# Softmax sums of 128 columns, a new order of steps at both ends and 47 added products in a gated attention block

## The chip, the cores and the metric

One core of a Trainium2 chip runs the whole kernel. The metric is the device time of one execution in microseconds. Three executions of the kernel before took 727.42, 727.99 and 729.45 us; the median is 727.99.

## What is computed

For 16 sequences of 256 tokens with 512 features, a gated cross-attention with 16 heads of 32 (keys and values from a context of 128 features) and a gated feed-forward net of width 1408, whose inputs and weights are rounded to fp8 values:

```python
scores = jnp.einsum('bhqd,bhkd->bhqk', qh, kh) * inv_sqrt_d
causal = jnp.tril(jnp.ones((sq, sk), dtype=bool))
scores = jnp.where(causal, scores, jnp.finfo(scores.dtype).min)
attn = jax.nn.softmax(scores, axis=-1)
...
x = x + jnp.tanh(g_xattn[0]) * _L0_xattn_ref(_layernorm(x, axis=-1), ctx_512, ...)
x = x + jnp.tanh(g_ffn[0]) * _L0_ffn_ref(_layernorm(x, axis=-1), L0_ffn_w_gate, ...)
...
scale_x = jnp.max(jnp.abs(xr), axis=1, keepdims=True) / FP8_MAX
qx = _fp8(xr / scale_x)
w_scale = jnp.max(jnp.abs(Wr), axis=1, keepdims=True) / FP8_MAX
qw = _fp8(Wr / w_scale)
y = qx * scale_x @ (qw * w_scale).T * scale
```

## The kernel before

The work goes by batches b of 256 tokens, in two halves t of 128. Of each batch, the layer norm of x and the context are split into a high and a low bf16 part and turned by a transposing DMA (`turn_x`). TensorE makes keys, queries and values from them in three bf16 products each. The high and low parts of keys and queries (the low ones made on POOL: `keys_low`, `queries_low`) are stacked by DMAs (`stack_keys(b, i)`, `stack_queries(b, i)`, i = 0 and 1 the high parts, 2 the low part) into K4 and Q4, from which one product gives exact scores.

`scores(b, c)`, for the pair c of heads (8 pairs), makes 768 columns: two heads times three blocks of 128, since of the four blocks of a causal 256 x 256 matrix one is empty. VectorE takes their row maxima (`maxima(b, c)`, L3116) and joins the two blocks of the second half (`second_maxima(b)`, L3121). POOL splits the maxima in three bf16 parts (`max_parts`), TensorE turns them (`turned_maxima`, L1349), ScalarE and a DMA bring them into Q4, and `shifted(b, c)` makes the scores again, transposed and less the maximum. ScalarE takes the exponential into the tile PT (`exps`), POOL clears the upper triangle (`causal_part`, L793), and `weighted(b, g)`, for a group g of four heads, multiplies with the values (L1411) and with `pick` (L1416), whose ones put the sum of the probabilities of head 4g+j into a row of `sum_bank`, a PSUM tile that all four groups add up in. `sums_inverted` (L3125) takes the reciprocal, `inverse_spread` (L3130, L3131) copies the row of each group g to all 32 rows of its block with a stream shuffle, `normalised` (L3136) multiplies, and `projected` makes the output projection. `residual` adds it to x. Then come the second layer norm, the rounding of x, the gate and up products (L1153), silu, the rounding of the product t, the down products, `down_scaled` (L3447), the addition and the store.

The weights of the feed-forward net are made ready ahead of and between the first batches, in 16 units: 0 to 3 are the rows of the down weights (128 x 1408 each), 4 to 15 pairs of 128 rows of gate or up weights. A unit u is loaded (`unit_loaded(u)` on SP's queue, L363 and L365), its row maxima taken on VectorE (`unit_maxima`, L2962), inverted and scaled (`pair_inverse`, `pair_scales`, L2982 and L2989), floored (L2947), lifted (L3056), rounded (L2943 on VectorE, L705 on POOL) and turned by TensorE (`unit_turned`, L1216). The attention weights are split as well (`attention_weights`, low parts on POOL, L779). POOL scatters the turned down rows to DRAM in 11 indirect DMAs (`down_placed`, L673).

The order of all this is written out by hand: for each of the engines and for SP a list of steps, run in order, with a wait on a semaphore in a step where it needs another engine. SP's list starts at L473. Every list has a loop `for k in range(1, 9)` in its middle for the steady batches. A step that waits holds up all behind it in its list. For example, a load of a unit of gate or up weights waits for the VectorE rounding that frees its room:

```python
            unit_loaded(7)
            stack_keys(0, 2)
            stack_queries(0, 0)
```

Here `unit_loaded(7)` waits for the fourth VectorE rounding, and `stack_keys(0, 2)` for the second `keys_low`.

## Time and profile before

| | |
|---|---|
| median of three executions | 727.99 us |
| profiled execution, its own time | 729.19 us |
| its span | 727.4 us |
| mean granted clock of TensorE | 0.978 |
| TensorE busy | 657.9 us (90%), 6091 instructions |
| VectorE busy | 680.1 us (93%), 1127 instructions |
| ScalarE busy | 555.5 us (76%) |
| POOL busy | 538.5 us (74%) |
| chain that ended last | TensorE 47%, VectorE 29%, POOL 11%, DMA 5%, issue 3%, ScalarE 3% |

The span is what the profiler saw from the first to the last instruction; the execution's own time has 1.8 us more around it. Busy shares are means over a beginning in which weights are prepared and batches 0 and 1 run, a steady middle, and an end without new batches. In the rows below PE is TensorE, DVE is VectorE, ACT is ScalarE, and `[2.02 <-DMA Q<-kl]` behind a row says how long the engine had stood idle before it and what released it.

### The profile page before, as it was taken

To read this page: it belongs to the slowest core of one execution; us is meant where nothing else is said; L and a number is where in the kernel's file an instruction comes from. 1 tells how busy PE (TensorE), PEld (TensorE's weight loads), DVE (VectorE), ACT (ScalarE), POOL (GpSimd) and SP (SyncE) were. 2 spreads that over 40 slices of the span, in tenths; PEclk is the share of its full clock that TensorE was granted. 3 is DMA by queue.
4 is the path that set the end of the run, shared out by engine and by line. 5 is a ranking of instruction groups with operands and counts; after the bars stand their busy time and mean duration, and the time that the engine had idled before them with its cause. 6 is when DMAs were issued, how large, how long until landed. Compare 5 with 4: busy or idle time off the path is not lost.

```text
span 727.4 us, 15637 instructions
## 1 busy us (share of the span) xinstructions
PE 657.9 (90%) x6091; PEld 419.9 (58%) x6160; DVE 680.1 (93%) x1127; ACT 555.5 (76%) x995; POOL 538.5 (74%) x601
## 2 busy tenths in 40 slices
PE   1758698999999999999999999999999999998794
PEld 1647476666566666566565657566566556545342
DVE  4999998989899999999999999999999999999997
ACT  6896878987869787878878787979797867555642
POOL 6768889796968778687878686968696677666651
PEclk9888999999999999999999999999999999999997
DMA  8887768385795757585867566675775686512121
GB/s 303 223 153 199 157 147 176 80 176 94 123 158 107 152 105 154 80 181 96 167 108 141 111 144 116 132 144 114 155 123 116 90 150 100 111 22 87 27 70 58
DMA packets 143479, 93.57 MB, mean 129 GB/s; under 512 B 107598, under 2 KB 114126, under 8 KB 143406
## 3 DMA queue, kind: packets, MB, share of 16 engines
q1 hardware_dynamic: 141246, 90.74, 61.6%
q0 software_dynamic: 576, 1.45, 0.8%
q8 instruction: 48, 0.79, 0.5%
q10 hardware_dynamic: 1584, 0.39, 0.3%
q14 instruction: 25, 0.20, 0.1%
HBM read 31.59 MB, written 9.83 MB: 57 GB/s over the span
## 4 chain that ended last, share of the span: by engine, by line
PE 47%; DVE 29%; POOL 11%; DMA 5%; issue 3%; ACT 3%; SPq 0%; ACTq 0%; DVEq 0%
PE pair L1153 26%; DVE mx L3116 5%; POOL PT L793 4%; PE pair L1411 4%; PE pair L1416 3%; DVE room L2943 2%; DVE room L2947 2%; PE pair L1394 2%; DVE room L3260 2%; PE pair L1440 2%; DVE room L3308 2%; PE pair L1436 2%; POOL room L832 2%; DVE tm L3323 2%; DVE wmax L2962 2%
## 5 line engine op out<-in xcount | busy, mean ns | idle before, releaser
L832 POOL TENSOR_TENSOR room<-room,up_scale 128x512 f32<-128x512 f32 (+1 forms) x96 | 125.6, 1312 | 63.1 <-ACT room L2349 62.2
L3116 DVE TENSOR_REDUCE mx<-pair 128x6 f32<-128x768 f32 x128 | 117.6, 947 | 1.7 <-PE pair L1343 1.4
L793 POOL TENSOR_SCALAR_AFFINE_SELECT PT<-PT 128x512 f32<-128x512 f32 x128 | 104.0, 841 | 13.1 <-ACT PT L2274 13.0
L2274 ACT ACTIVATE PT<-pair 128x768 f32<-128x768 f32 x128 | 98.3, 814 | 9.4 <-PE pair L1394 7.8
L1153 PE MATMUL pair<-WgT,room 128*128 128x512 bf16 (+1 forms) x382 | 89.5, 366 | 2.5 <-DVE room L3447 0.8
L1153 PE MATMUL pair<-xT,WqTh 128*128 128x256 bf16 x512 | 86.5, 272 | 1.5 <-ACT WdT L2037 1.3
L1153 PE MATMUL pair<-WuT,room 128*128 128x512 bf16 (+1 forms) x368 | 84.8, 361 | 3.3 <-DVE room L3260 1.4
L2349 ACT ACTIVATE room<-room,sx 128x512 f32<-128x512 f32 (+1 forms) x96 | 65.2, 682 | 24.2 <-DVE room L3260 18.8
L1153 PE MATMUL pair<-WdT,room 128*128 128x512 bf16 x326 | 75.4, 379 | 3.1 <-DMA room<-room 2.9
L2381 ACT ACTIVATE room<-room 128x512 bf16<-128x512 f32 (+1 forms) x96 | 55.8, 586 | 21.2 <-DVE room L3308 21.1
L1153 PE MATMUL pair<-xT,WqTl 128*128 128x256 bf16 x256 | 69.7, 272 | 0.0
L3308 DVE TENSOR_TENSOR room<-pair,room 128x512 f32<-128x512 f32 (+1 forms) x96 | 60.4, 638 | 6.0 <-POOL x L839 2.4
L3260 DVE TENSOR_TENSOR room<-pair,gate_scale 128x512 f32<-128x512 f32 (+1 forms) x96 | 60.3, 637 | 1.9 <-PE pair L1153 1.3
L839 POOL TENSOR_TENSOR x<-room,x 128x512 f32<-128x512 f32 x31 | 44.8, 1445 | 23.3 <-DVE room L3447 23.1
L1153 PEld LDWEIGHTS pair<-WuT,room 128*128 128x128 bf16 x384 | 36.9, 98 | 35.1 <-DVE room L3260 2.0
L1341 PE MATMUL pair<-K,Q 125*128 125x128 bf16 x256 | 51.4, 224 | 6.1 <-DMA Q<-kl 3.6
L1411 PE MATMUL pair<-PT,V 128*32 128x256 f32 (+1 forms) x1024 | 54.3, 329 | 2.4 <-POOL PT L793 2.2
L2943 DVE TENSOR_TENSOR room<-room 128x1408 bf16<-128x1408 f16 (+4 forms) x46 | 55.4, 1205 | 0.2
L1153 PEld LDWEIGHTS pair<-WdT,room 128*128 128x128 bf16 x330 | 31.7, 98 | 40.3 <-issue 2.9
L1153 PEld LDWEIGHTS pair<-WgT,room 128*128 128x128 bf16 x384 | 35.7, 98 | 32.9 <-ACT room L2037 1.8
L1153 PEld LDWEIGHTS pair<-xT,WqTh 128*128 128x128 bf16 x512 | 48.8, 98 | 9.2 <-ACT WdT L2037 1.6
L1416 PE MATMUL pair<-PT,pick 128*32 128x256 f32 (+1 forms) x1024 | 53.5, 326 | 0.0
(151 smaller groups left out, 1863.4 us busy)
## 6 DMA issues: line engine op xcount, KB each, us to landing
xin<-in_x_dram SPq DMA_DIRECT2D x16, 512.0 KB, 4.0
x<-in_x_dram SPq DMA_DIRECT2D x16, 512.0 KB, 4.8
K<-kh SPq DMA_DIRECT2D x32, 256.0 KB, 4.9
Q<-qh SPq DMA_DIRECT2D x32, 256.0 KB, 4.6
out_dram<-x SPq DMA_DIRECT2D x15, 512.0 KB, 3.0
K<-kl SPq DMA_DIRECT2D x16, 256.0 KB, 6.1
Q<-kl SPq DMA_DIRECT2D x16, 256.0 KB, 4.2
room<-in_L_ffn_w_down_dram SPq DMA_DIRECT2D x4, 704.0 KB, 9.0
```

The costliest lines, as they stand in the source:

```text
L793: pool.affine_select(out=view, in_=view, compare_op=ALU.is_ge, fill=0.0, base=0, pattern=[[0, 2], [0, 2], [1, P]], channel_multiplier=-1). ...
L832: pool.tensor_tensor(g, g, up_scale[:, chunk(n)[1]], ALU.mult).then_inc(slw_done, 1)
L1153: last = pe.matmul(out_ap, lhs, rhs, start=(fresh and n == 0), stop=(n == len(terms) - 1), skip_group_check=not fresh)
L1411: pe.matmul(w[HD * j:HD * j + HD, t * P:S], V[:, t, (G * g + j) * HD:(G * g + j + 1) * HD], probabilities(b, 2 * g + j // 2, j % 2, t), st ...
L1416: last = pe.matmul(sum_bank[HD * j:HD * j + HD, t * P:S], pick[:, g, :], probabilities(b, 2 * g + j // 2, j % 2, t), start=(g == 0 and t = ...
L2274: act.activation(head_columns(ring(b, c), 0, 384), head_columns(shifted_pair[c][:, :], 0, 384), ACT.Exp, scale=SCALE).then_inc(exp_done, 1)
L2349: act.activation(g, g, ACT.Silu, scale=sx[:, chunk(n)[0]:chunk(n)[0] + 1]).then_inc(silu_done, 1)
L2381: act.activation(qt[:, t, f], T[:, t, f], ACT.Abs, scale=TOKEN_LIFT).then_inc(abst_done, 1)
L2943: return dve.tensor_tensor(dst, w, high, ALU.subtract)
L3116: dve.tensor_reduce(mx[:, heads, :], head_columns(w, 0, 3 * P).rearrange("p h (r s) -> p h r s", s=P), AX.X, ALU.max).then_inc(max_done, 1)
L3260: dve.tensor_tensor(gs[:, n % 3, 0:width(n)], gate_bank[n][:, 0:width(n)], gate_scale[:, f], ALU.mult).then_inc(gs_done, 1)
L3308: dve.tensor_tensor(T[:, t, f], up_bank[n][:, 0:width(n)], gs[:, n % 3, 0:width(n)], ALU.mult).then_inc(t_done, 1)
```

## The change

1. **The sums.** A group's probabilities are 256 columns for keys of the first half (first and second half of the queries) and 128 columns for keys of the second half. Before, they were summed into a row for 256 queries, by four products of 256 columns and four of 128. Now each of them is summed by products of 128 columns, twelve in a group, into different rows of a `sum_bank` of 128 columns (row 4t + g of a block of 32; `pick` has a matrix for every t and g). The reciprocal works on 128 x 128, and eight stream shuffles of 128 columns spread it.
2. **Products nobody reads.** `kept_busy(b, n)` makes n products of 512 columns into a bank that is overwritten later: 9, 24, 8 and 6 of them, in TensorE's list up to `shifted(0, 0)`. Two explicit waits are ahead of the 24 and the 8.
3. **The order.** Every engine's list and the waits in it are written anew ahead of the loop and behind it. The loops have the same steps in the same order. SP's first loads are x, unit 0, context instead of context, unit 0, x; the residual's x of batch 0 comes much later; `unit_loaded(7)` comes behind `stack_keys(0, 2)`; the stacking of batch 1's low keys comes directly behind its high ones. POOL's `queries_low(1, .)` come ahead of `causal_part(0, 0)`, its scatters later and four in a row ahead of `max_parts(2)`. VectorE's maxima of batch 1 stand together.

The diff, cut to these places (the lists of ScalarE and the parts behind the loops are left out, as are the waits that follow from the order):

```diff
-        pick = sb("pick", [P, KT, HD])
+        pick_flat = sb("pick_flat", [P, TT * KT * (HD + 1)])
...
-        rsum = sb("rsum", [P, S])
+        rsum = sb("rsum", [P, P])
...
+        pick = pick_flat[:, 0:TT * KT * HD].rearrange("p (v c) -> p v c", c=HD)
+        pick_ones = pick_flat[:, :].rearrange("p (v c) -> p v c", c=HD + 1)
...
-            constant(pool.memset(pick[:, :, :], 0.0))
-            for g in range(KT):
-                constant(pool.memset(pick[:, g, :].rearrange("p (a b) -> p a b", b=4)[:, :, g:g + 1], 1.0))
+            constant(pool.memset(pick_flat[:, :], 0.0))
+            for a in range(HD // (TT * KT)):
+                constant(pool.memset(pick_ones[:, :, TT * KT * a:TT * KT * a + 1], 1.0))
...
+            def kept_busy(b, count):
+
+                for _ in range(count):
+                    pe.matmul(bank[b][:, 0:H], identb[:, :], WkvTh[:, 0:H], start=True, stop=True)
+
...
-                for t in range(TT):
-                    for j in range(G):
-                        last = pe.matmul(sum_bank[HD * j:HD * j + HD, t * P:S], pick[:, g, :],
-                                         probabilities(b, 2 * g + j // 2, j % 2, t), start=(g == 0 and t == 0),
-                                         stop=(g == KT - 1 and t == TT - 1), skip_group_check=True)
+                for j in range(G):
+                    pe.matmul(sum_bank[HD * j:HD * j + HD, 0:P], pick[:, g, :], probabilities(b, 2 * g + j // 2, j % 2, 0)[:, 0:P],
+                              start=(g == 0), stop=False, skip_group_check=True)
+                for j in range(G):
+                    pe.matmul(sum_bank[HD * j:HD * j + HD, 0:P], pick[:, KT + g, :], probabilities(b, 2 * g + j // 2, j % 2, 0)[:, P:S],
+                              start=False, stop=False, skip_group_check=True)
+                for j in range(G):
+                    last = pe.matmul(sum_bank[HD * j:HD * j + HD, 0:P], pick[:, KT + g, :], probabilities(b, 2 * g + j // 2, j % 2, 1),
+                                     start=False, stop=(g == KT - 1), skip_group_check=True)
...
-                dve.reciprocal(rsum[:, :], sum_bank[:, 0:S]).then_inc(rsum_done, 1)
+                dve.reciprocal(rsum[:, :], sum_bank[:, 0:P]).then_inc(rsum_done, 1)
 
             def inverse_spread(b, h):
                 if h == 0:
                     dve.wait_ge(rsum_done, b + 1)
-                dve.stream_shuffle(out=R[:, 2 * h, :], in_=rsum[:, :], mask=[2 * h] * HD)
-                dve.stream_shuffle(out=R[:, 2 * h + 1, :], in_=rsum[:, :], mask=[2 * h + 1] * HD).then_inc(r_spread, 1)
+                for g in range(2 * h, 2 * h + 2):
+                    for t in range(TT):
+                        last = dve.stream_shuffle(out=R[:, g, tok(t)], in_=rsum[:, :], mask=[KT * t + g] * HD)
+                last.then_inc(r_spread, 1)
...
             load_w_kv()
+            load_x(0)
+            unit_loaded(0)
             load_c(0)
-            unit_loaded(0)
-            load_x(0)
             unit_loaded(1)
             unit_loaded(2)
             unit_loaded(3)
             load_w_q()
-            load_x1(0)
-            load_c(1)
             turn_x(0, 0)
             load_x(1)
             turn_x(0, 1)
+            load_c(1)
             load_w_out()
             unit_loaded(5)
+            stack_keys(0, 0)
+            stack_keys(0, 1)
+            unit_loaded(4)
             unit_loaded(6)
-            stack_keys(0, 0)
-            unit_loaded(4)
-            stack_keys(0, 1)
+            stack_keys(0, 2)
             unit_loaded(7)
-            stack_keys(0, 2)
             stack_queries(0, 0)
-            load_c(2)
-            turn_x(1, 0)
             stack_queries(0, 1)
             stack_queries(0, 2)
+            turn_x(1, 0)
+            load_c(2)
             turn_x(1, 1)
-            unit_loaded(8)
             load_x(2)
             unit_loaded(9)
+            unit_loaded(8)
             unit_loaded(10)
             stack_keys(1, 0)
             unit_loaded(11)
             stack_keys(1, 1)
+            stack_keys(1, 2)
             stack_queries(1, 0)
+            stack_queries(1, 1)
             load_c(3)
-            stack_keys(1, 2)
+            load_x1(0)
+            unit_loaded(14)
+            no_maxima(2)
+            stack_queries(1, 2)
...
             attention_weights_low(1)
-            x_low(0, 1)
+            attention_weights_low(5)
+            attention_weights_low(3)
             attention_weights_low(4)
-            attention_weights_low(5)
             attention_weights_low(2)
-            attention_weights_low(3)
+            keys_low(0, 0)
             scales1(1)
-            keys_low(0, 0)
             keys_low(0, 1)
             c_low(1)
             x_low(1, 0)
             queries_low(0, 0)
+            queries_low(0, 1)
             x_low(1, 1)
-            queries_low(0, 1)
+            attention_weights_low(7)
             unit_rounded(5)
+            unit_rounded(7)
             keys_low(1, 0)
-            unit_rounded(7)
-            down_placed(2)
-            attention_weights_low(8)
+            keys_low(1, 1)
             c_low(2)
-            down_placed(0)
-            keys_low(1, 1)
             max_parts(0)
             scales1(2)
             unit_rounded(9)
+            x_low(2, 0)
+            queries_low(1, 0)
+            queries_low(1, 1)
...
             keys(0, 0)
+            keys(0, 1)
+            kept_busy(2, 9)
+            unit_turned(1)
+            values(0, 0)
             unit_turned(2)
-            keys(0, 1)
-            unit_turned(1)
             attention_weights(9)
-            values(0, 0)
+            queries(0, 0)
             unit_turned(0)
-            queries(0, 0)
             queries(0, 1)
+            attention_weights(7)
             queries(0, 2)
             queries(0, 3)
+            attention_weights(8)
             unit_turned(3)
+            spread(1)
             values(0, 1)
-            attention_weights(8)
             attention_weights(6)
-            spread(1)
-            attention_weights(7)
-            spread(2)
-            unit_turned(4)
+            pe.wait_ge(v_done, 2)
+            kept_busy(2, 24)
             scores(0, 0)
             scores(0, 1)
-            unit_turned(6)
+            scores(0, 2)
+            spread(2)
+            scores(0, 3)
+            unit_turned(4)
             keys(1, 0)
-            scores(0, 2)
-            scores(0, 3)
             keys(1, 1)
             scores(0, 4)
             scores(0, 5)
             unit_turned(5)
+            pe.wait_ge(w_taken, 5)
+            kept_busy(1, 8)
...
             queries(1, 3)
+            kept_busy(5, 6)
             shifted(0, 0)
...
             unit_maxima(4)
+            put_keys(0)
             pair_inverse(2)
-            put_queries(1)
+            unit_maxima(6)
             pair_scales(2)
-            unit_maxima(6)
-            unit_floored(4)
-            unit_lifted(4)
             unit_maxima(7)
-            unit_rounded(4)
             pair_inverse(3)
             pair_scales(3)
...
             unit_floored(11)
             unit_lifted(11)
+            unit_maxima(14)
             sums_inverted(0)
             inverse_spread(0, 0)
             inverse_spread(0, 1)
...
             maxima(1, 1)
             maxima(1, 2)
             maxima(1, 3)
-            unit_maxima(14)
             maxima(1, 4)
             maxima(1, 5)
-            unit_maxima(12)
-            pair_inverse(6)
             unit_maxima(15)
             maxima(1, 6)
+            pair_inverse(7)
             maxima(1, 7)
+            pair_scales(7)
+            second_maxima(1)
```

How the steps stand in the engines' queues, at three places. First SP's queue from the output projection's weights on; `room<-in_L_ffn_w_gate_dram` and `..._up_dram` are the loads of units 5 (gate), 6 (up), 4 (gate) and 7 (up). Before:

```order
L365 DMA room<-in_L_ffn_w_gate_dram 128x2x512 [waits w_round_dve]
L365 DMA room<-in_L_ffn_w_up_dram 128x2x512 [waits w_round_dve]
L428 DMA K_0<-kh 32x4x1024 [waits kh_done]
L365 DMA room<-in_L_ffn_w_gate_dram 128x2x512 [waits w_round_dve]
L428 DMA K_0<-kh 32x4x1024
L365 DMA room<-in_L_ffn_w_up_dram 128x2x512 [waits w_round_dve]
L428 DMA K_0<-kl 32x4x1024 [waits kl_done]
L437 DMA Q_0<-qh 32x4x1024 [waits qh_done]
```

Now:

```order
L363 DMA room<-in_L_ffn_w_gate_dram 128x2x512 [waits w_round_dve]
L420 DMA K_0<-kh 32x4x1024 [waits kh_done]
L420 DMA K_0<-kh 32x4x1024
L363 DMA room<-in_L_ffn_w_gate_dram 128x2x512 [waits w_round_dve]
L363 DMA room<-in_L_ffn_w_up_dram 128x2x512
L420 DMA K_0<-kl 32x4x1024 [waits kl_done]
L363 DMA room<-in_L_ffn_w_up_dram 128x2x512 [waits w_round_dve]
L433 DMA Q_0<-qh 32x4x1024 [waits qh_done]
```

The last of these loads, unit 7, stood ahead of `K_0<-kl` with its wait for kl_done and stands behind it now.

Second, VectorE from the normalisation of batch 0 to the second maxima of batch 1 (`mx<-mx`); `wmax<-room` are the maxima of units, `mx<-pair` those of scores. Before:

```order
L3136 TENSOR_TENSOR R<-pair,R 128x512 [waits r_spread] x2
L3116 TENSOR_REDUCE mx<-pair 128x2x3 [waits s_made] x4
L2962 TENSOR_REDUCE wmax<-room 128x2 [waits unit_in14]
L3116 TENSOR_REDUCE mx<-pair 128x2x3 [waits s_made] x2
L2962 TENSOR_REDUCE wmax<-room 128x2 [waits unit_in12]
L2982 RECIPROCAL winv<-wmax 128x3 [waits w_maxima]
L2962 TENSOR_REDUCE wmax<-room 128x1 [waits unit_in15]
L3116 TENSOR_REDUCE mx<-pair 128x2x3 [waits s_made] x2
L2989 TENSOR_SCALAR wmult<-winv 128x1 [waits w_inverse]
L2989 TENSOR_SCALAR wmult<-winv 128x1 x2
L3121 TENSOR_TENSOR mx<-mx 128x16 [waits max_done]
```

Now:

```order
L3276 TENSOR_TENSOR R<-pair,R 128x512 [waits r_spread] x2
L3254 TENSOR_REDUCE mx<-pair 128x2x3 [waits s_made] x6
L3091 TENSOR_REDUCE wmax<-room 128x1 [waits unit_in15]
L3254 TENSOR_REDUCE mx<-pair 128x2x3 [waits s_made]
L3113 RECIPROCAL winv<-wmax 128x3 [waits w_maxima]
L3254 TENSOR_REDUCE mx<-pair 128x2x3 [waits s_made]
L3133 TENSOR_SCALAR wmult<-winv 128x1 [waits w_inverse]
L3133 TENSOR_SCALAR wmult<-winv 128x1 x2
L3259 TENSOR_TENSOR mx<-mx 128x16 [waits max_done]
```

Two maxima of units (14 and 12) and one set of scales moved out from between the maxima of scores.

Third, TensorE in the first `weighted(0, 0)`, products with values and with `pick`. Before:

```order
L1411 MATMUL pair<-PT,V 32x256 [waits exp_done,cut_done]
L1411 MATMUL pair<-PT,V 32x256 x3
L1411 MATMUL pair<-PT,V 32x128 x4
L1416 MATMUL pair<-PT,pick 32x256 x4
L1416 MATMUL pair<-PT,pick 32x128 x4
```

Now:

```order
L1455 MATMUL pair<-PT,V 32x256 [waits cut_done,exp_done]
L1455 MATMUL pair<-PT,V 32x256 x3
L1455 MATMUL pair<-PT,V 32x128 x4
L1459 MATMUL pair<-PT,pick_flat 32x128 x4
L1462 MATMUL pair<-PT,pick_flat 32x128 x4
L1465 MATMUL pair<-PT,pick_flat 32x128 x4
```

The four sum products of 256 columns became eight of 128; the value products stay.

## Rows read from the trace of the kernel before

**Rows 1.** The windows by stage: stretch, its length, then busy us (instructions) by engine, clock, DMA

```profile
13.47:69.56 56.09, 36.69 (x289) 30.73 (x292) 55.18 (x75) 47.57 (x77) 42.16 (x34) 0.85 0.85 218
69.56:178.61 109.05, 97.88 (x1037) 66.71 (x1050) 102.16 (x171) 88.64 (x157) 91.56 (x99) 0.98 0.68 138
178.61:489.38 310.77, 305.74 (x2921) 196.28 (x2952) 294.02 (x497) 253.25 (x463) 242.59 (x273) 1.00 0.69 130
...
628.75:727.40 98.65, 79.16 (x514) 38.69 (x521) 92.11 (x169) 47.91 (x87) 50.00 (x48) 0.94 0.23 62
...
50.24:60.48 10.24, 7.83 (x57) 6.68 (x57) 10.21 (x16) 5.95 (x9) 4.50 (x3) 0.50 0.80 197
```

**Rows 2.** The chain that ended last, in order of time: start us, us, what

```profile
226.33 2.38 PE pair L1153 x11
...
264.80 2.38 PE pair L1153 x11
```

**Rows 3.** The timeline of TensorE: start us, us, what, [idle before <-releaser]

```profile
49.99 1.82 PE L1235 MATMUL pair<-ident,wmax 128*128 128x128 f32 x8 [2.79 <-ACT WoTh L2037]
...
54.69 0.29 PE L1341 MATMUL pair<-K,Q 125*128 125x128 bf16 x1 [2.02 <-DMA Q<-kl]
```

**Rows 4.** Windows of the sums' products (L1416) alone, in batch 6

```profile
314.87:315.30 0.43, 0.42 (x8) 0.27 (x12) 1.00 0.38 76
315.30:315.52 0.22, 0.22 (x12) 0.13 (x4) 1.00 1.02 208
```

**Rows 5.** VectorE groups by form: count | busy us, mean ns | idle before

```profile
L3125 DVE RECIPROCAL rsum<-pair 128x256 f32<-128x256 f32 x16 | 28.1, 1755 | 11.4 <-PE pair L1416 11.4
...
L2982 DVE RECIPROCAL winv<-wmax 128x4 f32<-128x4 f32 x4 | 0.7, 172 | 0.1
```

**Rows 6.** The timeline of VectorE: two shuffles of batch 6

```profile
319.22 0.45 DVE L3131 STREAM_SHUFFLE R<-rsum 128x256 f32<-128x256 f32 x1
...
319.57 0.45 DVE L3130 STREAM_SHUFFLE R<-rsum 128x256 f32<-128x256 f32 x1
```

**Rows 7.** The timeline of VectorE: maxima of batch 1

```profile
90.97 0.96 DVE L3116 TENSOR_REDUCE mx<-pair 128x6 f32<-128x768 f32 x1
93.06 2.90 DVE L3116 TENSOR_REDUCE mx<-pair 128x6 f32<-128x768 f32 x3 [1.14 <-PE pair L1343]
95.87 1.21 DVE L2962 TENSOR_REDUCE wmax<-room 128x2 f32<-128x1024 f32 x1
...
100.06 0.66 DVE L2962 TENSOR_REDUCE wmax<-room 128x1 f32<-128x512 f32 x1
...
102.36 0.27 DVE L2989 TENSOR_SCALAR wmult<-winv 128x1 f32<-128x1 f32 x3
102.55 0.17 DVE L3121 TENSOR_TENSOR mx<-mx 128x16 f32<-128x16 f32 x1
```

**Rows 8.** The timeline of TensorE: the end

```profile
706.63 2.54 PE L1153 MATMUL pair<-WuT,room 128*128 128x512 bf16 x12
713.77 0.61 PE L1538 MATMUL pair<-identb,room 128*128 128x128 bf16 x4 [4.59 <-DVE room L2943]
```

**Rows 9.** The timeline of VectorE: the start

```profile
11.08 1.22 DVE L2952 COPY Q<-rows_q 29x4096 bf16<-29x4096 bf16 x1 [1.09 <-POOL rows_k L866]
```

**Rows 10.** Line L365 (loads of gate and up units) from 30 to 50 us

```profile
DMA to landing us min/median/max: 4.6/4.7/4.7
```

**Rows 11.** The timeline of SP

```profile
42.00 0.56 SPq L428 DMA_DIRECT2D K<-kl  x1
```

**Rows 12.** The timeline of POOL

```profile
24.87 9.64 POOL L779 TENSOR_TENSOR WqTl<-x,WqTh 128x512 bf16<-128x512 f32 x4 [4.47 <-ACT WqTh L2037]
```

**Rows 13.** The timeline of VectorE: the preparation of units 4 to 7

```profile
42.36 1.56 DVE L2947 TENSOR_SCALAR room<-room,wmult 128x512 bf16<-128x512 bf16 x2
...
45.28 1.21 DVE L2962 TENSOR_REDUCE wmax<-room 128x2 f32<-128x1024 f32 x1
```

**Rows 14.** Line L673 (scatters of the down rows)

```profile
L673 POOL DMA_INDIRECT placed_down<-WdT,index x11: 963/1005/1124, 62.9 to 143.4; - x11
```

More of the change, by code:

```diff
@@ L834, in added @@
             def added(b, t):
+                if t == 0 and b == 0:
+                    pool.wait_ge(y_done, 1)
+                if t == 0 and b == 9:
+                    pool.wait_ge(y_done, 19)
                 if t == 0 and b >= 12:
@@ L944, in _ @@
             normalised_low(1, 1)
+            keys_low(3, 0)
             c_low(4)
-            keys_low(3, 0)
-            down_placed(9)
+            keys_low(3, 1)
+            down_placed(1)
+            down_placed(10)
+            down_placed(2)
+            down_placed(3)
+            max_parts(2)
             up_scaled(0, 0)
-            max_parts(2)
             up_scaled(0, 1)
+            scales1(4)
             up_scaled(0, 2)
-            keys_low(3, 1)
-            down_placed(10)
-            scales1(4)
+            queries_low(3, 0)
             up_scaled(0, 3)
+            up_scaled(0, 4)
             causal_part(2, 0)
@@ L975, in _ @@
             up_scaled(1, 0)
+            keys_low(4, 1)
             up_scaled(1, 1)
@@ L978, in _ @@
             up_scaled(1, 2)
+            scales1(5)
             up_scaled(1, 3)
-            keys_low(4, 1)
+            queries_low(4, 0)
+            queries_low(4, 1)
             up_scaled(1, 4)
-            scales1(5)
-            up_scaled(1, 5)
             causal_part(3, 0)
@@ L3860, in _ @@
             rounded_x(13, 1)
+            maxima(15, 0)
             sums_inverted(14)
```

2143 lines of the change are left out of this document (1125 added, 1018 removed).

## The prediction, made before the changed kernel ran

> **What bounds the kernel now.** The page's shares have TensorE and VectorE both busy for nine tenths of the span or more, which does not say which of them ends a wait. So I read the windows by stage, then the chain of waits, then single stretches. The windows tell the stages apart [rows 1]. From 13.47 to 69.56 VectorE works 55.18 of 56.09 us and TensorE 36.69: the preparation of weights on VectorE sets the pace. From 69.56 to 178.61 both have gaps, 11.17 us on TensorE and 6.89 on VectorE. From 178.61 to 489.38, batches 3 to 10, TensorE works 305.74 of 310.77 and VectorE has 16.75 us to spare: TensorE sets the pace, and the chain there is one row of products per turn, 38.47 us apart (226.33 to 264.80) [rows 2]. After 628.75, in the last batches, both have gaps again. The granted clock is 1.00 in the middle, 0.85 in the preparation and 0.50 from 50.24 to 60.48 [rows 1]; 0.50 is the level of 1.2 GHz, which followed two waits of TensorE, the later of them for the stacked queries [rows 3].
>
> The profiled execution took 729.19 us (span 727.4 and 1.8 around it), 1.2 above the median of three, 727.99. The sum is made against 729.19, and the result then taken from the median. A difference of 0.3%, 2.2 us, is about what a measurement of this kernel can tell from none.
>
> **1. Softmax sums of 128 columns.** Per group of four heads TensorE now issues 24 records in place of 16 (each product here leaves two). In columns nothing changes: before, two wide and two narrow rounds of four products side by side, 2 x 256 + 2 x 128 = 768 columns; now 6 x 128 = 768. Rows bear out that a record's time goes by columns: eight wide records fill 0.43 us, and 0.22 us hold the eight narrow ones (the row counts 12, since four before them reach in) [rows 4]. So the 0.43 + 0.22 = 0.65 us per group stays, cost 0. If a record cost the same whatever its width, 0.65 / 16 = 0.041 us, 24 would take 0.98, and 64 groups would cost +20.8 us: the upper bound, kept as a rival.
>
> VectorE gains. The reciprocal of 128x256 takes 1.755 us, that of 128x4 0.172 [rows 5]: 0.0063 us a column, so 128x128 takes 0.96, and 0.80 is saved in each of 16 batches. The four shuffles start about 0.345 us apart (319.22, 319.57), 1.38 for all [rows 6]. No row shows one of 128 columns. Bounds: purely by columns eight cost the same, purely by instruction +1.38. Small instructions follow each other every 0.09 us (three in 0.27 [rows 7]); with 0.09 of each 0.345 fixed, eight take 8 x (0.09 + 0.128) = 1.74, +0.36. Net per batch -0.44, between -0.80 and +0.58; I take -0.44, nearest to the column side, since 0.345 for 256 columns is itself far above 0.09. The Trainium skill (Perfetto Trace Analysis, Optimizing Scalar/DVE Operations) speaks against splitting: about 60 ns of overhead per VectorE instruction on SBUF; by that figure four more cost 0.24, and the net would be an estimated -0.56. No row here shows the overhead by itself.
>
> What is it worth? In batches 3 to 10 VectorE already has 16.75 us to spare [rows 1]: 0, hidden behind TensorE; that cover would have to go first. In the last four batches the reciprocal stands between the last sums and the projection, with both engines short of work: 4 x 0.44 = 1.8 us. The epilogue's other swaps change who waits by fractions in 19.5 us of TensorE gaps after 628.75 [rows 1], of which one wait alone, for VectorE's rounding, is 4.59 [rows 8]; nothing shortens that rounding. I give them -0.7; bounds 0 (they only permute) and -2.5. **Epilogue: -2.5.**
>
> **2. Products nobody reads.** 47 of 512 columns. Twelve products of 512 columns take 2.54 us at full clock [rows 8], 0.212 each, so 10.0 us in all. All stand in waits: the nine behind keys(0, 1) and the 24 ahead of scores(0, 0), where TensorE waited 2.79 and 2.02 us [rows 3]; the rest ahead of a wait too. They run in order, so 24 x 0.212 = 5.1 us are free only if their release (v_done) comes 5 us before the stacked queries. What they could give is the clock: 50.24 to 60.48 at 0.50, where TensorE works 7.83 us and VectorE 10.21 of 10.24 [rows 1]. VectorE is the bound there, so a faster TensorE gives nearly nothing in that stretch: 0. Bounds: -1.0, and +5.1 if the 24 delay the scores entirely.
>
> **3. First down unit earlier.** On SP's queue it now stands behind x0 (512 KB) where it stood behind c0 (128 KB), so it is not fetched earlier at all: the change does not do what its name says here. Behind its maximum VectorE stood 1.09 us, until 11.08, for a constant of POOL [rows 9]. There is room for a landing 1.09 us later, and I cannot tell from a row how much later it will be. 0; bounds 0 and +1.
>
> **4. Unit 7 behind a wait.** Before, SP issued unit 7 and then waited for kl_done with K_0<-kl; such a load lands 4.6 to 4.7 us after its issue [rows 10]. Now K_0<-kl stands ahead, and unit 7 queues behind its wait on POOL's keys_low(0, 1). The wait ended and the issue began at 42.00, and took 0.56 [rows 11]. The first of POOL's two key steps now stands ahead of the layer norm's scale steps, so I put kl_done at 40 to 42. Plus 0.6 for the issue and 4.7 for the landing: 45.3 to 47.3. VectorE, whose floor and lift of unit 4 moved behind this maximum (2.97 us, 42.36 to 45.28), asks at 42.3 for what came up at 45.28 before [rows 13]. Idle 3 to 5 us, of which the moved 2.97 are the earlier asking; the net delay is 0 to 2.0 and I take **+1.0**.
>
> **5. From the sums of batch 0 to the second maxima of batch 1.** Before, VectorE took 11.58 us from 90.97 to 102.55, with a wait of 1.14, three unit maxima (1.21, 1.21, 0.66) and small scale steps between the eight maxima of 0.865 [rows 7]. In the new order one unit (0.66) is left between, the others stand ahead or behind: 8 x 0.865 + 0.66 + 0.45 = 8.0 us, **-3.6**, if TensorE and the stacked queries keep up. They are meant to: K_1<-kl is issued right behind the high keys, where it stood behind a wait for the queries and a load of context, and POOL's queries_low(1, .) come ahead of the first causal parts instead of behind the sixth and eighth. This is a move, not a saving: units 12 and 13 are paid later, in the 6.89 us of VectorE gaps of the stage [rows 1]. Bounds: 0 if the whole is paid back, -6.9 if every gap of the stage closes as well. Four of the scatters of down rows now stand in a row ahead of max_parts(2): POOL spends 1.0 us on each [rows 14], and it had 17.5 us of gaps in the 109.05 [rows 1]: 0, bound +2, half of the four.
>
> **Sum:** epilogue -2.5, products 0, unit 7 +1.0, batch 1 -3.6, steady turns 0: -5.1. 729.19 - 5.1 = 724.1 for the profiled execution, and from the median 727.99 - 5.1 = **722.9**.
>
> **Rivals.**
> - *Unit 7 makes it slower.* If kl_done comes later than I think, VectorE stands still with nothing behind it on its queue that could go ahead. The sum crosses zero when unit 7 lands 5.1 us beyond the 46.3 assumed, at 51.4; that is kl_done at 46.1. With kl_done at 48.6, 2.5 us beyond, the time is 730.5. For it: four low parts of the query weights at 2.41 us stand ahead on POOL, and their waits on ScalarE moved. Against: POOL had 4.47 us idle before them [rows 12], and kl_done came at 42.00. Chance 0.09.
> - *No change.* The batch 1 gain is paid back by units 12 and 13 and by scatters on POOL, since from 178.61 on TensorE sets the pace and only its own products count; the epilogue keeps the reciprocals, -1.8, of which half is hidden, -0.9: 727.1. For it: TensorE lacked only 11.17 us in the stage, with the steady pace directly behind. Chance 0.18.
> - *More than forecast.* The clock stays up from 50 to 60 us, so scores(0, .) come sooner, and all of VectorE's 6.89 us of gaps in the stage close: -6.9, with the reciprocals of batches 0 and 1 -0.9, the epilogue -2.5, unit 7 +1.0, in all -9.3: 718.7. Against: VectorE lacked only 0.91 us in the preparation [rows 1], so a sooner TensorE finds it busy. Chance 0.20.
> - *Records cost by number.* +20.8 on the sum: 743.7. Against it is the narrow half of [rows 4]. Chance 0.01. The Trainium skill (TensorE: Matmul & The Clock Gate, "Wait — 56ns, not 53.3ns?") has two floors for small products: about 25 ns from start to start, and about 62 ns each when the sequencer's microcode decodes them. By the second, 24 x 0.062 = 1.49 us per group, an estimated +54 us; the rows, 16 in 0.65 us, are already faster than it allows. By the first, 0.60 us, below the 0.65 kept here.
>
> **Numbers.** The forecast has 0.52. Its own range is -8 to -2.5: 720.0 to 725.5. With the larger gain and the no-change case, each with a spread of 1.3 to 1.5, the range becomes 717.5 to 728.5; outside it are the slower cases (0.10) and tails of the others. Faster by over 2.2 us: 0.52 + 0.20 = 0.72; same 0.18; slower 0.10.
>
> **What would show it.** Right: reciprocals of 128 columns near 0.96 us and shuffles near 0.22 apart; sums of a group still 0.65 us; 38.5 us from turn to turn; second maxima of batch 1 near 99 us instead of 102.55; a landing of unit 7 at 45 to 47. Wrong: VectorE idle over 5 us before unit 7's maximum; turns longer than 38.47, then the sums cost TensorE; the distance to the first steady turn unchanged, then the start was only permuted; products nobody reads ending after the data they wait for.

## The result and the profile after

The changed kernel is slower: 732.11 us (median of 7) against 728.02 us (median of 7 of before, on the same chip), a ratio of 1.0051 with the interval 1.0038 to 1.0065. The forecast was 722.9, and its range ended at 728.5. The profiled execution took 732.13 us with a span of 730.4, 3.0 us above the span before.

I compare by the starts of `turned_maxima(b)` on TensorE, "mark b" below, in us from the span's start. Mark 3 is where the steady turns begin, mark 11 where they end.

| profiled kernel | mark 0 | mark 1 | mark 2 | mark 3 | mark 11 | mark 11 to the end |
|---|---|---|---|---|---|---|
| before | 69.6 | 104.0 | 139.7 | 178.6 | 489.4 | 238.0 |
| changed | 69.1 | 103.5 | 142.5 | 181.5 | 489.6 | 240.8 |

Up to mark 1 the change gains half a microsecond, and then loses 3.3 to mark 2. The steady part hides this in this pair: its turns are 38.49 (38.47 before), but the profiled execution of before had two longer turns (40.1 and 39.9) that the changed one did not have. The end, from mark 11 on, costs 2.8.

The windows by stage, of the changed kernel, in the order of [rows 1] (cut at its own marks; columns as there). The last row is a stretch in the new end:

```profile
13.47:69.06 55.59, 41.79 (x332) 30.86 (x333) 51.97 (x74) 47.55 (x79) 38.08 (x31) 0.97 0.85 202
69.06:181.50 112.44, 101.77 (x1151) 69.24 (x1152) 103.06 (x197) 88.22 (x157) 92.02 (x102) 0.97 0.75 145
181.50:489.60 308.10, 308.09 (x3209) 202.02 (x3208) 291.51 (x561) 253.16 (x463) 241.50 (x272) 1.00 0.68 130
...
631.50:730.40 98.90, 78.61 (x549) 38.91 (x547) 90.30 (x186) 47.43 (x86) 49.53 (x46) 0.94 0.24 55
50.24:60.48 10.24, 8.50 (x87) 6.40 (x86) 10.24 (x17) 6.39 (x11) 4.25 (x2) 1.00 0.98 176
637.33:640.74 3.41, 3.41 (x13) 1.63 (x14) 3.36 (x4) 0.26 (x2) 2.03 (x2) 0.50 0.00 0
```

The preparation runs at a granted clock of 0.97 instead of 0.85, and 50.24 to 60.48 at 1.00 instead of 0.50: the products nobody reads hold the clock here (`no_fill` below has the stretch back without them). In other profiles of the same order one stretch of 3.4 us at 1.2 GHz is left, 47.9 to 51.3 in `after_c5`. The steady part is pure TensorE, 308.09 of 308.10 us. From 69 to 181 VectorE has 9.38 us of gaps where it had 6.89 [rows 1]. From 637.33 to 640.74 TensorE works without a gap at 1.2 GHz; before ran at full clock there, but had such a stretch from 691.9 to 695.4 that the changed kernel did not have.

VectorE's groups by form, against [rows 5] (the line of the reciprocal is L3263 now, of the shuffles L3270), and two of the shuffles in the timeline, against [rows 6]:

```profile
L3263 DVE RECIPROCAL rsum<-pair 128x128 f32<-128x128 f32 x16 | 15.3, 956 | 10.8 <-PE pair L1465 10.7
```

```profile
89.55 0.29 DVE L3270 STREAM_SHUFFLE R<-rsum 128x128 f32<-128x128 f32 x1
...
89.76 0.30 DVE L3270 STREAM_SHUFFLE R<-rsum 128x128 f32<-128x128 f32 x1
```

The chain in the steady part has the sums of a group as three rows of 0.22 us:

```profile
195.29 0.22 PE pair L1459 x8
195.51 0.22 PE pair L1462 x8
195.73 0.22 PE pair L1465 x8
```

Here the forecast held: 0.956 us, shuffles 0.21 apart, 0.65 us per group. So did the landing of unit 7: VectorE waits for it until 46.92 (forecast 45.3 to 47.3).

The loss between marks 1 and 2 begins in the next rows. First VectorE in the changed kernel at 108 us (L3049 is the floor, L3283 the residual), and what TensorE waits for (L1428 is `shifted(1, 4)`, whose bank is that of the output projection):

```profile
107.97 5.78 DVE L3049 TENSOR_SCALAR room<-room,wmult 128x512 bf16<-128x512 bf16 x2
113.67 0.74 DVE L3283 SCALAR_TENSOR_TENSOR x<-pair,tanh_g,x 128x512 f32<-128x512 f32 x1
```

```profile
114.48 0.23 PE L1428 MATMUL pair<-Q,K 99*128 99x128 bf16 x1 [3.86 <-DVE x L3283]
```

The two floors take 5.78 us; the first takes 0.34 (107.97 to 108.31), the second 5.52. Behind TensorE's wait of 3.86 us its clock falls beside full work. That stretch of the changed kernel, and the whole way from mark 1 to mark 2 in the changed kernel and in before:

```profile
115.10:118.50 3.40, 3.40 (x27) 1.88 (x29) 3.11 (x5) 2.76 (x5) 1.42 (x2) 0.50 0.05 5
103.50:142.50 39.00, 33.63 (x379) 22.71 (x379) 33.87 (x64) 29.66 (x56) 29.88 (x36) 0.96 0.62 111
104.00:139.70 35.70, 32.54 (x352) 22.12 (x356) 33.07 (x54) 29.73 (x55) 30.24 (x33) 1.00 0.68 138
```

So TensorE is idle for 5.37 us between the marks where it was idle for 3.16, and busy for 33.63 where it was busy for 32.54: together the 3.3 us. The 3.40 us at 1.2 GHz alone cost about 1.7 us, an estimate from half the clock. POOL in the same stretch:

```profile
107.65 1.25 POOL L673 DMA_INDIRECT placed_down<-WdT,index  x1 [0.17 <-ACT qh L2108]
108.94 2.27 POOL L774 TENSOR_TENSOR kl<-exact,qh 128x512 bf16<-128x512 f32 x2
111.17 0.66 POOL L723 TENSOR_TENSOR xcat<-cin,xcat 128x256 bf16<-128x256 f32 x1
111.79 2.45 POOL L819 TENSOR_SCALAR_AFFINE_SELECT PT<-PT 128x512 f32<-128x512 f32 x4
```

POOL ran seven tensor steps without a gap, from 108.94 to 114.24, the causal parts at 0.61 us each, and VectorE's second floor ended only at 113.75, after six of them. In the kernel before, POOL's row at this place was as dense, but the two took turns: five causal parts in 5.87 us, 1.17 each, and no VectorE step beside the row above 2.2 (POOL first, then VectorE):

```profile
114.13 5.87 POOL L793 TENSOR_SCALAR_AFFINE_SELECT PT<-PT 128x512 f32<-128x512 f32 x5
```

```profile
111.84 1.31 DVE L2947 TENSOR_SCALAR room<-room,wmult 128x512 bf16<-128x512 bf16 x2
113.08 2.17 DVE L2943 TENSOR_TENSOR room<-room 128x1024 bf16<-128x1024 f32 x1
115.17 1.12 DVE L3056 SCALAR_TENSOR_TENSOR room<-room,wmult 128x512 f32<-128x512 f32 x1
```

### The profile page after: what moved, and what is told of

It is laid out like the page before. It is cut to its first block, busy times and chain, and to the rows that moved or that the text cites. A ratio compares the mean times of both kernels' runs of the same rounds, so it can differ in the third digit from the quotient of the medians.

```text
span 730.4 us, 16944 instructions
## 1 busy us (share of the span) xinstructions
PE 671.0 (92%) x6719; PEld 432.1 (59%) x6719; DVE 675.2 (92%) x1255; ACT 553.9 (76%) x995; POOL 540.2 (74%) x601
## 4 chain that ended last, share of the span: by engine, by line
PE 59%; DVE 18%; POOL 11%; ACT 6%; DMA 3%; issue 2%; SPq 1%; ACTq 0%; DVEq 0%
PE pair L1183 32%; PE pair L1455 5%; PE pair L1492 3%; PE pair L1493 3%; PE pair L1488 2%; PE pair L1429 2%; DVE room L3049 2%; POOL PT L819 2%; DVE room L3455 2%; DVE mx L3254 2%; PE pair L1376 2%; PE pair L1378 2%; PE pair L1377 2%; DVE room L3508 2%; PE pair L1428 1%
## 5 line engine op out<-in xcount | busy, mean ns | idle before, releaser
L858 POOL TENSOR_TENSOR room<-room,up_scale 128x512 f32<-128x512 f32 (+1 forms) x96 | 127.2, 1331 | 62.8 <-ACT room L2439 62.5
L2366 ACT ACTIVATE PT<-pair 128x768 f32<-128x768 f32 x128 | 98.4, 815 | 13.7 <-PE pair L1429 8.7
L1183 PE MATMUL pair<-WuT,room 128*128 128x512 bf16 (+1 forms) x384 | 88.3, 361 | 0.7 <-DVE rsum L3263 0.5
L828 POOL TENSOR_TENSOR ol<-R,oh 128x512 bf16<-128x512 f32 x32 | 36.6, 1157 | 26.5 <-ACT oh L2108 26.5
L1428 PE MATMUL pair<-Q,K 99*128 99x128 bf16 x256 | 48.7, 223 | 7.3 <-DVE x L3283 3.9
L1376 PE MATMUL pair<-K,Q 125*128 125x128 bf16 x256 | 49.9, 220 | 5.7 <-DVE R L3276 4.2
L1183 PEld LDWEIGHTS pair<-WdT,room 128*128 128x128 bf16 x330 | 31.9, 98 | 39.2 <-DMA room<-room 2.8
L869 POOL TENSOR_TENSOR x<-room,x 128x512 f32<-128x512 f32 x31 | 42.4, 1369 | 16.1 <-DVE room L3584 16.1
```

Of the source, the lines that this page charges most:

```text
L858: pool.tensor_tensor(g, g, up_scale[:, chunk(n)[1]], ALU.mult).then_inc(slw_done, 1)
L1183: last = pe.matmul(out_ap, lhs, rhs, start=(fresh and n == 0), stop=(n == len(terms) - 1), skip_group_check=not fresh)
L1376: pe.matmul(w[:, tok(4 * h)], q[0:MASK_END, head, 0:P], k[0:MASK_END, head, 0:P], start=True, stop=True)
L1428: pe.matmul(w[:, tok(4 * h)], K4[b % 2][0:99, head, P:S], Q4[b % 2][0:99, head, P:S], start=True, stop=True)
L2366: act.activation(head_columns(ring(b, c), 0, 384), head_columns(shifted_pair[c][:, :], 0, 384), ACT.Exp, scale=SCALE).then_inc(exp_done, 1)
```

## Experiments

My theory: the sums gain a little; the new order ahead of the loop loses about 3 us through the held floor; the new order behind it loses as much again. The rivals: the sums' extra instructions cost it, or one of the two ends alone, or the way the moved loads meet the transposing DMAs.

**The reference.** All kernels of this section have the 92 transposing DMAs replaced by plain ones of the same bytes. The tiles are then not turned, so these kernels compute something else in the same steps:

```diff
-                sp.dma_start_transpose(xT[:, :, tok(t)], xcat[:, t, :]).then_inc(xT_in, 16)
+                sp.dma_start(xT[:, :, tok(t)], xcat[:, t, :].rearrange("p (k s) -> p k s", s=P)).then_inc(xT_in, 16)
```

> The kernel before with each of its 92 transposing DMAs replaced by a plain DMA of the same tile and the same bytes (pieces of 256 bytes), so the operands of the products are not turned; all else is the same. It is the reference for the runs that follow, which have the same replacement. Turns of 38.5 us in the middle as before, the whole within 5 us of 728.0, since TensorE and VectorE set the pace and a copy should land about as fast as a transposition (3.4 to 3.8 us in the trace).

Measured: 727.87 us (10 runs) against 727.58 of the kernel before, ratio 1.000 (0.9987 to 1.0013); turns of 38.47. The replacement is neutral for before, and what follows can be read against before itself.

**The change taken apart.** `after_c5` is the changed kernel. `sums_c5` is before with the sums alone. `begin_c5` has the sums, the changed lists ahead of the loop (with the waits that belong to them) and before's lists behind it; `end_c5` the reverse. The loops are the same in both kernels. The cut in each engine's list:

```diff
 # begin_c5, every engine
+            <list of the changed kernel>
             for k in range(1, 9):
                 ...
-            <list of the changed kernel>
+            <list of the kernel before>
```

> The changed kernel with the same replacement (each of the 92 transposing DMAs a plain copy of the same bytes). The kernel before with it took 727.9 us, as without it (727.6). Theory 1 (the new orders cost the time through TensorE's wait for VectorE at 114 us and through the end, not through the transpositions): 3 to 5 us above that, 731 to 733, again with one VectorE floor of several us beside a row of POOL steps near 108 us. Rival (the loss lies in how the transpositions meet the moved loads and stacking DMAs): within 1 us of 727.9.

> With the same replacement: sums of 128 columns, the changed order ahead of the loop (with its 47 products nobody reads), the order of before behind the loop. Theory 1 (the first part loses near 3 us where one VectorE floor stood 5.5 us beside POOL and TensorE waited 3.9 us for it; the end loses about as much again): 729 to 731, the floor long again. Rival 1 (the whole loss is in the end): 726.4 to 727.9. Rival 2 (the sums cost it all): as after_c5.

> With the same replacement: sums of 128 columns, the order of before ahead of the loop, the changed order behind it. Theory 1: the end alone costs, 729 to 730.5. Rival 1 (the end costs all): as after_c5. Rival 2 (the end costs nothing, the beginning all): 726.4 to 727.9.

> With the same replacement: the sums of 128 columns alone (products, reciprocal, eight shuffles), every order as before. Theory 1 (the two new orders cost the time, the sums gain a little in the last batches): 726 to 727.5. Rival (the eight more products of a group and the four more shuffles cost more than the shorter reciprocal gives): 730 to 732.

| kernel | median us (runs) | ratio to before (interval) | mark 1 | mark 2 | mark 11 to the end |
|---|---|---|---|---|---|
| before_c5 | 727.9 (10) | 1.0000 (0.9987 to 1.0013) | 104.6 | 140.3 | 239.2 |
| after_c5 | 732.1 (8) | 1.0056 (1.0042 to 1.0071) | 104.2 | 143.4 | 241.0 |
| begin_c5 | 733.7 (4) | 1.0079 (1.0059 to 1.0098) | 104.3 | 144.3 | 238.6 |
| end_c5 | 730.8 (9) | 1.0023 (1.0006 to 1.0039) | 107.4 | 143.4 | 240.1 |
| sums_c5 | 725.7 (10) | 0.9974 (0.9953 to 0.9996) | 104.1 | 143.3 | 237.6 |

The changed kernel is as slow with plain copies, so the rival of the transposing DMAs falls. The sums alone are a gain, so the first rival falls too. Added to the sums alone, each new order costs: with the new beginning it is 733.7 (729 to 731 was expected), with the new end 730.8, against 725.7. The two do not add up (8.0 and 5.0 against the 6.4 of both), and behind the new beginning the new end shows no cost in the times: after_c5 is 1.6 below begin_c5, with intervals that overlap.

Executions of one kernel differ by 6 to 7 us here (sums_c5: 723.7 to 729.8), and the profiled ones of sums_c5 and end_c5 took 729.4 and 735.0, which shows in their marks 1 and 2; so a mark of one profile counts only where it repeats. In sums_c5 TensorE waited 1.73 and 2.04 us near 121 and 125, then worked at 1.2 GHz from 126.7 to 130.1, and the distance from mark 1 to mark 2 is 39.2 without a held step; in the same kernel once more (`sums_again` below) it is 35.3. What repeats: the held floor, 5.52 us in the changed kernel, after_c5 and begin_c5 and in no kernel with the old beginning; and, less clearly, the end, 240.1 and 241.0 us with the new lists, 238.6 and 237.6 with the old.

**The held floor.** `residual_first` moves the residual ahead of it; `scatter_between` leaves VectorE alone and moves one of POOL's scatters (`down_placed(0)`, 1.25 us) between the two `queries_low(2, .)`. Both are read against `after_again`, the changed kernel with the plain copies once more.

```diff
 # residual_first, VectorE
+            residual(0, 1)
             unit_floored(12)
-            residual(0, 1)
 # scatter_between, POOL
-            down_placed(0)
             queries_low(2, 0)
+            down_placed(0)
             queries_low(2, 1)
```

> The changed kernel with the plain copies once more, as the reference of this call: 731 to 733 us, with the VectorE floor of 5.52 us and TensorE's wait of 3.9 to 4.0 us behind it, as in three profiles so far.

> after_again with one VectorE step moved: residual(0, 1) ahead of the floors of unit 12. Theory 1 (a VectorE floor that meets a row of POOL steps without a gap is held until the row has a gap, and TensorE waits since the residual stands behind it): the second product of the projection is ready near 109.5 us, the residual ends near 110.3, TensorE's wait of 3.9 us goes, the floors behind it are held again but end at the same time as before (near 114), about 3.5 us long; total 3 to 4 us less, 728 to 729.5. Rival (the wait is only passed on, since TensorE meets the next wait for POOL or VectorE): within 1 us of after_again.

> [...] Theory 1 (the floor is held as long as POOL's row of tensor steps has no gap): the floor gets in during the scatter and takes 0.5 to 2 us instead of 5.52, TensorE's wait of 3.9 shrinks below 1, total 2.5 to 4 less. Rival 1 (the floor is slow for a reason of its own, such as a late input): still 5.5 long, total unchanged. Rival 2 (a POOL scatter holds VectorE just as tensor steps do): still over 4 long.

Measured: after_again 732.7 (6 runs, 732.0 to 737.3; floor 5.52, wait 4.01), residual_first 732.5 (6 runs), scatter_between 733.5 (4 runs). Neither gained, where I had expected 2.5 to 4 us. What failed is the expected total, not the place. In residual_first TensorE's wait of 3.9 is gone, the floor is held 4.61 us and ends at 116.1, and TensorE waits later, for VectorE's maxima(2, 0), again with 3.4 us at 1.2 GHz behind it (126.5 to 129.9):

```profile
111.47 5.25 DVE L3049 TENSOR_SCALAR room<-room,wmult 128x512 bf16<-128x512 bf16 x2
```

```profile
125.91 1.18 PE L1270 MATMUL pair<-ident,wmax 128*128 128x128 f32 x6 [4.37 <-DVE mx L3254]
```

In scatter_between both floors are through by 110.01, the second in 0.34 us beside the scatter, but the lift behind the residual is held in its place (5.33 of the 6.95 us of the two):

```profile
108.50 1.50 DVE L3049 TENSOR_SCALAR room<-room,wmult 128x512 bf16<-128x512 bf16 x2
...
110.85 6.95 DVE L3198 SCALAR_TENSOR_TENSOR room<-room,wmult 128x512 f32<-128x512 f32 x2
```

```profile
109.76 1.11 POOL L673 DMA_INDIRECT placed_down<-WdT,index  x1 [0.16 <-issue]
110.89 1.17 POOL L774 TENSOR_TENSOR kl<-exact,qh 128x512 bf16<-128x512 f32 x1
112.01 0.68 POOL L723 TENSOR_TENSOR xcat<-cin,xcat 128x256 bf16<-128x256 f32 x1
112.63 4.62 POOL L819 TENSOR_SCALAR_AFFINE_SELECT PT<-PT 128x512 f32<-128x512 f32 x7
```

So a floor is not slow by itself: in these three orders whichever of these VectorE steps came up beside POOL's row was held, through six or seven of POOL's steps. It was not held to the end of the row: in the changed kernel the floor ended at 113.75 and the row at 114.24, in residual_first at 116.08 and 116.57. Nor does a scatter let every step through: in the changed kernel the second floor came up at 108.23, with 0.68 us of a scatter still to run, and was held all the same. What ends the holding is open. The Trainium skill (SBUF — State Buffer, "SBUF: two separate sides") says that VectorE and GpSimd share a port pair as an exclusive lock, that the loser is fully blocked for the whole instruction, and that a VectorE operation takes part in it when it is in a two-port mode, or has two SBUF inputs while the GpSimd step reads SBUF. The trace agrees with the blocking and shows more: here VectorE was blocked for six GpSimd steps in a row, 4.7 us, where before it got in after one.

`gaps` puts scatters into the row, on top of residual_first:

```diff
-            down_placed(5)
             x_low(3, 0)
-            down_placed(0)
             queries_low(2, 0)
+            down_placed(5)
             queries_low(2, 1)
+            down_placed(0)
             c_low(3)
             causal_part(1, 0)
             causal_part(1, 1)
+            down_placed(9)
             causal_part(1, 2)
...
             unit_rounded(13)
-            down_placed(9)
```

> residual_first with three of POOL's scatters put between its tensor steps: x_low(3, 0), queries_low(2, 0), scatter, queries_low(2, 1), scatter, c_low(3), two causal parts, scatter. Theory (VectorE steps get in where POOL's row has a scatter): no VectorE step above 2.7 us between 100 and 125, the time from turned_maxima(1) to turned_maxima(2) falls from 39.2 to 39.6 us to 37 to 38.5, total 1 to 2 below the 732.1 to 732.7 of after. Rival (the time lies in VectorE's deferred unit maxima and their floors, not in the held step): 39 or more, total as before.

Measured: 729.9 (10 runs), ratio 1.0022 (1.0003 to 1.0041), where after_c5 has 1.0056 (1.0042 to 1.0071) and residual_first 1.0063 (1.0037 to 1.0088). From mark 1 to mark 2 it takes 37.8 us instead of 39.2 to 39.6, and the longest VectorE step there is 2.60. The expectation came true, the total by a little more. So 2.3 to 2.9 us of the whole came back against the two medians of the changed kernel (2.5 to 3.9 by the ratios), with no tensor step added or left out. That speaks for the cost of holding; but the scatters moved also let POOL's queries_low(2, .) start sooner (107.78, where the changed kernel has 108.94), and the two effects were not separated. It is not all of the loss: before takes 35.7 between these marks. TensorE now waits for the causal parts, which stand behind the scatters, and 3.4 us at 1.2 GHz follow once more (114.9 to 118.3):

```profile
115.09 0.65 PE L1455 MATMUL pair<-PT,V 128*32 128x256 f32 x4 [2.34 <-POOL PT L819]
```

**Unit 7.** `unit7_early` puts `unit_loaded(7)` back ahead of `stack_keys(0, 2)` in the changed kernel.

> The changed kernel with unit_loaded(7) ahead of stack_keys(0, 2) again, as in the order of before. Theory (the wait for unit 7, 2.5 us in every profile of the changed order, is free, since VectorE's steps met less of POOL's meanwhile and TensorE's chain stands elsewhere): within 1 us of 732.1 to 732.7. Rival (the wait is a part of the loss): 1.5 to 2.5 less.

Measured: 734.8 (4 runs, 733.4 to 738.0), mark 0 at 70.0. VectorE's wait of 2.5 us for unit 7 is gone (one of 1.0 us, for ScalarE, comes in its place) and nothing is won: it is 2 us slower than after_again, outside the expected 1 us, for a reason that was not looked for. Nothing here makes the wait that I feared a part of the loss.

**The products nobody reads.** `no_fill` leaves all 47 out of the changed kernel, with their two waits. `sums_fill` puts 30 of them into the old order, on top of the sums:

```diff
             unit_turned(4)
+            pe.wait_ge(v_done, 2)
+            kept_busy(2, 24)
             scores(0, 0)
...
             queries(1, 3)
+            kept_busy(5, 6)
             shifted(0, 0)
```

> after_again without the 47 products nobody reads and the two waits ahead of them. Theory 1 (they lie in waits of TensorE, and the clock that they keep up is worth little while VectorE sets the pace): within 1 us of after_again, with a stretch at 1.2 GHz back near 50 us. Rival 1 (they delay the scores by up to 5.1 us): 727 to 729. Rival 2 (the clock is worth several us): 734 or more.

> sums_again with 30 of the products nobody reads at their places in TensorE's old order: 24 ahead of scores(0, 0) (with the wait for v_done) and 6 ahead of shifted(0, 0). Theory (they hold TensorE at 2.4 GHz where it waits for VectorE, as in the changed kernel, where leaving them out cost 6 us): no stretch at 1.2 GHz from 50 to 60 us, and 0.5 to 2.5 us less than sums_again. Rival (VectorE sets the pace there in the old order, 10.2 of 10.2 us, so nothing comes of the clock): within 0.7 of sums_again. It is the candidate that may beat both kernels.

no_fill: 738.9 (4 runs: 734.6, 738.4, 739.5 and 739.9) against 732.7 of after_again. So in the changed order the products are worth 6.2 us by the medians and 3.3 by the ratios (1.0122, 1.0084 to 1.0160, and 1.0076, 1.0050 to 1.0103); I had priced them at nothing. Without them the clock falls beside work, in the windows of no_fill:

```profile
51.31:58.14 6.83, 4.49 (x31) 4.17 (x32) 6.11 (x11) 2.61 (x5) 4.20 (x2) 0.50 1.07 196
64.97:68.38 3.41, 3.26 (x25) 2.70 (x24) 3.38 (x4) 3.41 (x7) 3.02 (x4) 0.50 1.03 241
195.57:201.50 5.93, 5.93 (x19) 2.67 (x20) 1.02 (x2) 0.38 (x1) 1.04 (x3) 0.50 0.01 3
```

Mark 0 comes at 71.0 instead of 68.9, mark 2 at 146.1 instead of 142.4, and mark 3 still 3.7 later. The third row stands behind a wait of 2.96 us for a DMA, seen in this one profile; that turn took 5.9 us more, and whether this belongs to the missing products is open. So of the 7.8 us by which this profile is longer than that of after_again, 3.7 are tied to the missing products.

sums_fill: 738.4 (5 runs, 736.6 to 745.0), 13.7 above the same kernel without the products, where I had expected a gain. The wait for v_done ends at 54.81 in the old order, when the queries are already stacked, and the 24 products stand between them and the scores:

```profile
54.81 4.87 PE L1108 MATMUL pair<-WkvTh,identb 128*128 128x512 bf16 x11 [2.09 <-ACT V L1985]
59.91 2.98 PE L1108 MATMUL pair<-WkvTh,identb 128*128 128x512 bf16 x12 [0.22 <-issue]
```

Half of them run at 1.2 GHz, 7.9 us in all; mark 0 comes at 76.5 instead of 69.5. That is 7.0 of the 21.3 us by which this profile, the longest of the five, exceeds that of sums_again; behind mark 11 it takes 243.8 us with the old lists, with a wait of 4.49 us for a DMA at 629, and why is open. In the changed order the same products begin at 47.87 and the scores at 53.06, 1.6 earlier than before [rows 3].

**The version that beats both.** `sums_again`, before with the sums alone:

> The order of before with the sums of 128 columns alone, once more, with more rounds: 725 to 727, 1.5 to 3 below the kernel before; the reciprocals of the last four batches and what follows gain 1.6 us between the last steady turn and the end (237.6 us in the first profile, 239.2 with the old sums).

Measured: 724.8 (8 runs), ratio 0.9956 (0.9937 to 0.9975), and 235.9 us behind mark 11. By the ratio it beats before by about 3.2 us (0.44%; by the medians 4.4) and the changed kernel by about 7. This is with the plain copies, under which before keeps its time; with the transposing DMAs it was not measured.

## Why the prediction was wrong

The forecast was 5.1 us faster; it became 4.1 slower. Two steps failed. The -3.6 for batch 1 counted what left VectorE's row and not what the new order put in the way of TensorE: a held VectorE step, a wait of 3.86 us and 3.40 us at 1.2 GHz, 3.3 us lost where 3.6 were to be gained. And the new end, priced at -0.7, brought two new waits and costs time. By the prediction's own steps:

- **Softmax sums: right.** Durations and the group's 0.65 us came as worked out: 0.80 us less for the reciprocal and 0.27 more for the shuffles (8 x 0.206 against 4 x 0.345; the two sizes leave 0.067 a shuffle that does not go by columns, an estimate, where 0.09 was put), -0.53 a batch where -0.44 was put. "Epilogue: -2.5" had -1.8 for them; the sums alone gave 1.9 and 3.2 us of the whole by the ratios. Behind mark 11 the two profiles have 237.6 and 235.9, and before 238.0 and 239.2.
- **"The epilogue's other swaps ... I give them -0.7": the wrong sign.** Added to the sums alone the new end costs 5.0 us of the median; by the marks it is about 2.4 (241.0 against 238.6, 240.1 against 237.6), but over all profiles with the new sums the two ends overlap: 238.4 to 241.0 in nine with the new lists, 235.9, 237.6, 238.6 and 243.8 (sums_fill) with the old. VectorE's `normalised` stands in front of scores that lost the products ahead of them, and TensorE waits there, in rows that [rows 8] did not have:

```profile
555.99 0.22 PE L1376 MATMUL pair<-K,Q 125*128 125x128 bf16 x1 [1.42 <-DVE R L3276]
```

```profile
635.17 0.23 PE L1376 MATMUL pair<-K,Q 125*128 125x128 bf16 x1 [1.82 <-DVE R L3276]
```

  Behind the second wait comes the stretch at 1.2 GHz with TensorE at work (637.33 to 640.74 above). All nine profiles of the new end have the two waits; six have the stretch (240.1 to 241.0 us behind mark 11), three have not (238.4 to 239.2). That the missing products ahead of the scores cause the waits is read from the lists and not shown; no run puts them back. In the pair of this document the stretches at 1.2 GHz behind mark 11 add up to the same (10.3 us, before 10.4), so there the clock explains little of the 2.8 us.
- **"-3.6" from batch 0's sums to batch 1's second maxima: right on VectorE, then overpaid.** The eight maxima did close up (92.18 to 100.75, 8.6 us, against 90.97 to 102.55 [rows 7]), but mark 1 gained only 0.5, and units 12 and 13, "paid later, in the 6.89 us of VectorE gaps", were paid ahead of maxima(2, 0), where TensorE waits. The bound "0 if the whole is paid back" was too good: it lacked the case that the moved steps meet POOL's row and are held, and that TensorE's clock falls behind the wait that this makes. All eight profiles with a step held over 4 us have a wait of TensorE of 3.86 to 4.37 us and 3.4 or 6.8 us at 1.2 GHz around or behind it. `gaps` gave back 2.3 to 2.9 us; how holding, the clock, the deferral and POOL's scatters share the loss was not separated.
- **"Products nobody reads: 0": right that they cost nothing, wrong that they give nothing.** The argument was that VectorE is busy 10.21 of 10.24 us there; the worth came later, 2.1 us by mark 0 and 3.7 by mark 2 in the profiles, 3.3 to 6.2 of the whole. It lowers the loss, so the two failed steps cost more than the total shows.
- **"Unit 7: +1.0"**: the landing came as described, the wait was 2.5 us where 3 to 5 were put (the moved steps are 2.92 us by its rows, not 2.97), and taking it away gained nothing.
- **First down unit: 0.** It landed 1.41 us later (9.78 against 8.37), 0.32 more than the room it had, and mark 0 is no later for it.
- Slower had 0.10. Its rival, "unit 7 makes it slower", named the wrong mechanism for the right side. Nearer was "no change" (0.18), which had the gain of batch 1 paid back; it stopped at paid back.

## What to carry to other kernels

A reordering is not priced by the waits it removes: sum up for every engine what stands ahead of the next step that the bounding engine needs, and look which steps of VectorE and GpSimd will run side by side after the move. A change that bundles a shorter computation with a new order should be timed apart; here the computation alone was the gain. Products that keep the clock up helped here where their release came well ahead of the data that the next real product waits for, and cost 7 us where it did not. A new wait of the bounding engine can cost more than its length: look at the granted clock behind it.

## What the runs showed of the hardware

- One VectorE step of 0.34 us took 5.52 us (5.520 to 5.531 in six profiles) beside a gapless row of GpSimd steps, six of them complete; nearly the same row made the two take turns before. What decides between the two is open.
- Beside an indirect DMA's issue on GpSimd (1.1 to 1.25 us) a VectorE floor passed in 0.34 us; a second floor that came up 0.6 to 0.7 us before the issue ended did not.
- Behind waits of TensorE of about 4 us it worked at 1.2 GHz for 3.4 us or more, in eight profiles of eight. A wait of 1.8 us was followed by such a stretch in six profiles of nine; with it the way from mark 14 to mark 15 took 41.5 to 41.9 us, without it 40.4.
